# Reordering the factorisation slot: where the channel sum, the updates, the additions and the splits stand in four engine queues

## The reference

```python
def nnmf_conv(x, w):                      # w normalised: wp; wt = wp transposed and flipped; 6 groups of 16 channels
    h = full(1 / 96)
    for _ in range(25):
        recon = conv2d(h, wt, 6)          # 3 x 3, grouped: "reconstruction"
        nu = x / maximum(recon, EPS)
        h = h * conv2d(nu, wp, 6)         # grouped: "correlation", then the update
        h = h / maximum(h.sum(axis=1), EPS)   # sum over all 96 channels
    return h
```

## Time and profile before

| what | value |
|---|---|
| median of the runs before (3 runs, 7553.3 to 7556.19) | 7554.52 us |
| the profiled execution: its own time, its span | 7552.64 us, 7550.9 us |
| busy over the span: PE, DVE, ACT, POOL | 86%, 73%, 61%, 62% |
| granted TensorE clock, mean over the span | 0.956 |
| the factorisation's four pairs, from about 2040 to 6746 us of the span | some 1180 us each |
| one ordinary slot of the loop, from sum to sum | 22.41 to 22.45 us |
| the first slot after each turn of TensorE's loop (5 per pair) | 27.0 to 28.4 us |

### The profile page before, as it was taken

How to read it: one execution, slowest core, us unless ns; L and a number is a source line. 1 busy time by engine, 2 the same in 40 slices (tenths; PEclk the granted TensorE clock), 3 DMA queues, 4 the chain that set the end, 5 groups by cost and what they waited for, 6 DMA issues and landing times. The chain is left out here.

```text
span 7550.9 us, 237789 instructions
## 1 busy us (share of the span) xinstructions
PE 6477.1 (86%) x97977; PEld 3568.9 (47%) x97977; DVE 5483.5 (73%) x8000; ACT 4590.7 (61%) x6901; POOL 4709.7 (62%) x3220
## 2 busy tenths in 40 slices
PE   7999999999588888888888878888878888866666
PEld 3444444444355555455555545555545555532222
DVE  5666666666588888778888868888868888865555
ACT  3444444444277777667777757777757777755554
POOL 3333333333188788768888767888767888863444
PEclk9999999999799999999999999999999999987778
DMA  0000000000100000000000010000010000011111
GB/s 15 20 22 24 17 24 20 22 24 16 37 3 3 3 3 3 31 11 3 3 3 3 3 39 3 3 3 3 3 39 3 3 3 3 3 45 38 50 50 38
DMA packets 92369, 119.74 MB, mean 16 GB/s; under 512 B 23696, under 2 KB 73136, under 8 KB 91568
## 3 DMA queue, kind: packets, MB, share of 16 engines
q1 hardware_dynamic: 91568, 106.87, 4.7%
HBM read 53.67 MB, written 52.79 MB: 14 GB/s over the span
## 5 line engine op out<-in xcount | busy, mean ns | idle before, releaser
L190 POOL TENSOR_TENSOR nn_hf<-nn_hf,nn_sr 128x512 f32<-128x512 f32 (+1 forms) x800 | 1444.3, 1828 | 807.7 <-DVE nn_sr L380 807.7
L464 PE MATMUL nn_P<-nn_hh,nn_w 64*64 64x256 f16 x38400 | 1565.2, 279 | 319.2 <-issue 86.9
L464 PEld LDWEIGHTS nn_P<-nn_hh,nn_w 64*64 64x64 f16 x38400 | 980.7, 108 | 1001.7 <-issue 948.3
L385 DVE SCALAR_TENSOR_TENSOR nn_P<-nn_P,nn_xs 128x612 f32<-128x612 f32 x1200 | 962.3, 802 | 546.9 <-PE nn_P L464 537.1
L471 PE MATMUL nn_P<-nn_nh,nn_w 64*64 64x512 f16 x19200 | 1276.1, 379 | 72.1 <-DVE nn_hf L371 9.3
L258 ACT ACTIVATE nn_yy<-nn_P 128x612 f32<-128x612 f32 x1200 | 810.2, 675 | 787.2 <-DVE nn_P L385 782.4
L1168 PE MATMUL at_PC<-at_xp,at_w1T 97*128 97x512 f16 x5184 | 1235.8, 383 | 0.0
L391 DVE TENSOR_TENSOR nn_P<-nn_P,nn_nh 128x612 f32<-128x612 f32 x1200 | 958.2, 798 | 123.7 <-ACT nn_nh L262 116.3
L396 DVE SCALAR_TENSOR_TENSOR nn_nl<-nn_P,nn_yy 128x612 f16<-128x612 f32 x1200 | 952.0, 793 | 88.4 <-ACT nn_yy L265 56.2
L464 PE MATMUL nn_P<-nn_hl,nn_w 64*64 64x256 f16 x19200 | 988.3, 274 | 0.0
L276 ACT ACTIVATE nn_hh<-nn_hf 128x512 f16<-128x512 f32 (+1 forms) x780 | 650.8, 834 | 523.9 <-POOL nn_hf L190 523.8
(11 more groups left out here) (210 smaller groups left out, 7742.0 us busy)
## 6 DMA issues: line engine op xcount, KB each, us to landing
xn_scratch<-at_xb SPq DMA_DIRECT2D x128, 114.8 KB
nn_xs<-xn_scratch SPq DMA_DIRECT2D x48, 306.0 KB, 4.5
at_x<-in_x SPq DMA_DIRECT2D x32, 384.0 KB, 3.2
x_scratch<-at_x SPq DMA_DIRECT2D x64, 192.0 KB, 2.1
h_scratch<-nn_hf SPq DMA_DIRECT2D x48, 256.0 KB, 2.8
ml_xt<-x_scratch SPq DMA_DIRECT2D x32, 384.0 KB, 4.7
ml_ht<-h_scratch SPq DMA_DIRECT2D x128, 96.0 KB
out<-ml_ot SPq DMA_DIRECT2D x64, 192.0 KB, 2.1
```

The costliest lines, as they stand in the source:

```text
L190: e.tensor_tensor(hf[c][:, g, :], hf[c][:, g, :], sr[:, :].unsqueeze(1).broadcast_to((128, g.stop - g.start, A_COLS)), ALU.mult).then_inc( ...
L385: e.scalar_tensor_tensor(Pv[k % 2], Pv[k % 2], EPS * H_SCALE * W_SCALE, half(xs[u][:, k, :, :].rearrange("p i n -> p (i n)")), ALU.max, AL ...
L464: return pe.matmul(out[:, 0:AC, rows_y] if near else out[:, 1:BC, rows_y], w1[rows, wp, a, 1 if near else 0, k, cols], (hh, hl)[dp][u][row ...
```

## The change

Three things move, with no instruction added or taken away.

- TensorE: SUM' goes behind R3 (it stood behind R2), and C0 goes directly behind it, ahead of R4.
- VectorE: N1 goes ahead of U4'; U4' and U5' are taken apart, with W2 between them; W3 goes ahead of N2.
- ScalarE: S3 waits until the whole inversion of group 1 is done, S1' until that of group 4 is done and group 5 has its high half. GpSimd: A2 goes to the end of its own slot; n3 goes ahead of A3'; LE0' goes ahead of n2'.

```diff
@@ GpSimd, slot @@
-                if depth:
-                    add(e, o, 2, s - 1)
                 if depth == 2:
                     low_late(e, u, 2, m, carry)
+                    normalise(e, u, 3, s - 1)
                 if depth:
                     add(e, o, 3, s - 1)
-                if depth == 2:
-                    normalise(e, u, 3, s - 1)
-                if depth:
                     add(e, o, 4, s - 1)
...
                     normalise(e, o, 1, s)
+                    low_early(e, o, 0, m)
                     normalise(e, o, 2, s)
-                    low_early(e, o, 0, m)
                 add(e, u, 1, s)
                 if depth:
                     low_early(e, o, 1, m)
+                add(e, u, 2, s)
@@ GpSimd, last @@
-                add(e, 1, 2, s - 1)
@@ ScalarE, slot @@
                 invert(e, 0, s, depth)
-                logarithm(e, 1, s, depth)
-                nu_high(e, 1, s)
+                invert(e, 1, s, depth)
                 if depth == 2:
                     split(e, u, 3, s - 1)
-                nu_full(e, 1, s)
...
-                logarithm(e, 4, s, depth)
-                nu_high(e, 4, s)
+                invert(e, 4, s, depth)
+                logarithm(e, 5, s, depth)
+                nu_high(e, 5, s)
                 if depth:
                     split(e, o, 1, s)
-                nu_full(e, 4, s)
-                invert(e, 5, s, depth)
+                nu_full(e, 5, s)
@@ VectorE, slot @@
                 nu_low(e, 0, s)
+                residual(e, 1, s)
+                nu_low(e, 1, s)
                 if depth:
                     update(e, o, 4, s - 1)
+                weigh(e, u, 2, s)
+                if depth:
                     update(e, o, 5, s - 1)
-                weigh(e, u, 2, s)
-                residual(e, 1, s)
-                nu_low(e, 1, s)
+                weigh(e, u, 3, s)
                 residual(e, 2, s)
                 nu_low(e, 2, s)
-                weigh(e, u, 3, s)
@@ TensorE, slot @@
-                    if k == 2 and depth:
-                        sum_up(e, 1 - u, s)
-                    if k == 4:
+                    if k == 3:
+                        if depth:
+                            sum_up(e, 1 - u, s)
                         correlate_pair(e, 0, s, not depth)
```

## The result

The changed kernel takes 7501.78 us (median of six runs, 7496.4 to 7506.13); six runs of the kernel before beside it gave 7555.35. The ratio is 0.9931, 95% interval 0.9921 to 0.9941: 53 us less, where 12 were predicted, and outside the predicted range. The profiled execution took 7505.59 us, its span is 7503.8 us, and the granted clock has a mean of 0.959.

What follows compares the result with a forecast made beforehand. The ring GpSimd, sum, ScalarE, VectorE was taken to bound the kernel. Ordinary slots -29, queue breaks +12, loop turns +10 and pair starts -5 gave -12 us: 7542 us, range 7527 to 7565.

Steps and rivals of the forecast that it cites:

- The ring that sets the slot: Ordinary slot: the waits GpSimd, sum, ScalarE, VectorE set its length, 22.42 us before and 22.25 us after the change.
- the 260 us of waiting: TensorE idle for GpSimd's additions ahead of all 200 channel sums, 260.1 us in all; claimed to be slack, not gain.
- The return leg: From the sum through clamp, logarithm and exponential to refine_sum's end: 5.87 us becomes 5.68, as the clamp is freed.
- The floor of the forward leg: GpSimd's eleven operations from `sr` to the sum: only their order differs, at least 16.55 us, taken as 16.57.
- TensorE's leg: TensorE's own way from `sr` to the sum, with R3 now ahead of it: 16.5 us, level with GpSimd's 16.55.
- The first rival: TensorE's way from `sr` to the sum is longer than added up: slot 22.53, +46, 7600 us; chance 0.25.
- The sign of being wrong: Prediction wrong if L378's starts are 22.4 or more apart, or GpSimd shows a gap ahead of LE1', LL2 or A4'.
- the turn of the loop: 20 slots where TensorE's loop branches: idle 4.01 us before R0 kept, sum later, net +0.55 each, +10 us.
- The breaks of TensorE's queue: Losses on TensorE's way to the sum, no longer covered by slack: 0.5 us per eight-slot body, 24 bodies, +12 us.
- the second rival: Breaks in TensorE's instruction queue do not reach the sum and the legs stay clear: -30, 7524 us; chance 0.17.
- The start of a pair: First slots of four pairs: N1 right behind N0 removes R3's 2.53 us wait; -1.3 each, -5 us.
- Moves at nothing: S3, S1', LE0' and A2 moved on ScalarE and GpSimd: later work covers the delays, booked at zero.

Runs made afterwards that it cites:

- n3_between: The changed kernel with GpSimd's n3 put back between A3' and A4': 7484.12 us, 0.9904 against the kernel before.

## Why the prediction was wrong

**What held.** The ring that sets the slot, GpSimd, sum, ScalarE, VectorE, and that the 260 us of waiting were slack: they fell to 51.9 us, and the ordinary slots gained 10.5 us. The return leg of 5.68. The floor of the forward leg: with n3 between the additions it is 16.56, and TensorE's leg, reckoned at 16.5, really is level with it: R5 waits 0.77 us for `nu_low` 3, and the sum 0.13 to 0.27 for GpSimd. The first rival (TensorE's leg longer) did not happen. The sign of being wrong that the prediction gave for the slot did not come either (starts of 22.4 or more apart); of the gaps on GpSimd there was one, the 0.08 us ahead of A4'.

**The step that failed: the turn of the loop.** "TensorE stands idle for 4.01 us before R0" was taken as a constant of the branch, and only the order behind it was reckoned, to +0.55 a turn. That reckoning was good: the two turns of the changed kernel that kept the long stall took 27.97 and 28.28, against 27.51 + 0.55 = 28.06. But the stall is no constant. It was some 1.4 us shorter in 18 turns, in which the last block of the straight code was fetched before the head's and not beside it. The idle increments ahead of the sum give the shorter stall in the same way without any change of order. In the sum: +11 for the order, 20 x (7.21 - 5.85) = -27 for R0's earlier start, and the remaining -9 lie with five turns of 24.8 to 25.0 us, of which more below. The measured term is -25 in place of +10, and this is the bulk of the miss. The Trainium skill (Runtime: NRT & Kernel Launch, Instruction fetch mechanics) says that a taken branch outside the window stalls; every turn here agrees. Whether the stall was near 2.7 us or 4.1 went with the neighbouring fetch.

**The forward leg** was mis-sized: "Only their order differs", 16.55 to 16.57, measured 16.68. The order of the same eleven operations is worth 0.12 us, over 168 slots about 20 us (-10.5 in place of -29); n3 between the additions gets it back (n3_between: 7484 us).

**The breaks of TensorE's queue**, +12, hardly arose. With n3 between the additions the ordinary slot has a mean of 22.26, and its two legs add up to 16.56 + 5.68 = 22.24. The third slot of a body is 0.08 longer than the others, 2 us in 24 bodies. In the order with C0 behind R4 the same slot cost 7 us, so the term hangs on the order. That breaks do not reach the sum was the condition of the second rival, whose time of 7524 us was out too, for the turns were wrong in it as well.

**The start of a pair** had the wrong mechanism. -1.3 each was put down to N1 right behind N0 "takes this wait away"; alone that gave nothing measurable, since R4 then waits for `nu_low` 2. N1's and C0's moves together gave 56.85 to 54.47, 57.73 to 54.93 and 57.15 to 54.50. The measured term is -10.8 in place of -5; of this 8.0 are the three stretches, and the 2.8 of the first pair may be chance, since in kernels with the old first slot the first start lay anywhere from 2073.4 to 2077.8.

**Moves at nothing.** Right for the change as it was made, but the reason given (room in the covers of single operations) hid that they are conditions: when VectorE wants `nu_low` 1 earlier, ScalarE's splits behind whole inversions are worth 410 us (7911.39 with their old places, 7501.78 with the new ones), and 809 us with GpSimd's old order (8294.06 and 7485.26).

The terms as measured, for the kernel with n3 between the additions: ordinary slots 28 (168 times 0.168), turns 550.2 - 519.5 = 31, starts 12 (first start 3.9 earlier, stretches 2.9, 3.7 and 2.0 shorter): 71 us. The medians differ by 71 us and the spans of the two profiled runs by 68.5, since the rest took 3 us more.

**Still open.** Why the last block is fetched 2.6 us earlier after the change. TensorE's loop has as many instructions in both orders, and with C0 behind R4 the early fetch is gone. In all kernels with eight slots in the body and without idle increments it goes with C0's place ahead of R4, and with R5's wait, which the same kernels have; no run separated the two. The idle increments show that the early fetch is possible with neither. Open too is how the overlap holds up R0.

## What to carry to other kernels

A stall at a loop's branch is not a constant of the loop: look in the DMA view at which instruction fetches lie in it (here 2.6 to 3.0 us of idle time or 4.0 to 4.5) before booking it as unchanged, and try a longer body or a few idle instructions where the engine has slack. Taking away a wait that is no bound where it is seen (TensorE's 260 us) brings nothing by itself, while work that fills a wait in a rare stretch, a first slot, pays in full. When parts of a reordering are tried one by one, expect the parts to be conditions of each other: here the new orders of three engines gave 0.9916 together, while without ScalarE's the kernel was 5% slower than before, without TensorE's 13%, and without C0's new place alone no faster.

## What was not expected of the hardware

- The 16 KB block of the loop's head takes 1.0 us to fetch alone and 2.1 us beside another one, and R0 comes some 2.0 us after it has landed (medians of 20 turns each; beside another one the distance went up to 2.9).
- TensorE's clock after a turn. Before, in every one of the 20 turns the granted clock fell to its lower level (1.2 GHz) around the start of R0, behind a stall of 4 us, and some 50 to 95 reconstruction matmuls ran at it. After a shorter stall it did not fall in 5 of 18 turns, and in 11 of 19 in the kernel with n3 between the additions; such turns took 24.8 to 25.6 us, the others 26.0 and more. The windows show the mean granted clock in the column behind POOL's, first before, 4005 to 4009, then in one of the five turns after, 4168 to 4172:

```profile
4005.00:4009.00 4.00, 3.73 (x76) 2.88 (x80) 1.39 (x2) 0.54 (x1) 0.68 (x1) 0.63 0.01 4
```

```profile
4168.00:4172.00 4.00, 3.81 (x108) 2.85 (x112) 1.82 (x3) 1.22 (x2) 4.00 (x3) 1.00 0.01 4
```

  Why it came in one turn and not in another with the same stall is open.
- An addition on GpSimd right behind the one whose result it reads started 0.08 us after that one's end, while operations that do not read their neighbour's result started 0.03 to 0.05 us before it. With another operation between the two additions the same work took 0.12 us less. That the reading is the reason fits every pair in these rows, but no run tests it by itself.
- An increment of a semaphore ahead of R0 costs 0.09 us on TensorE's queue (twelve of them 1.1 us, where there had been no gap).
